# A graph network on one core: edge messages by outer products instead of per-edge matrices

## The reference, cut to what matters

```python
eh  = relu(e_feat @ en1_w.T + en1_b)            # (edges, 128), once
w_e = (eh @ en2_w.T + en2_b).reshape(-1, 32, 32)
for _ in range(6):
    msg = einsum('ei,eio->eo', out[src], w_e)
    agg = segment_sum(msg, dst) + conv_bias
    out = h = gru_cell(relu(agg), h)
```

## Time and profile before

| | us |
|---|---|
| median of 3 runs | 42728.8 (42723.92 to 42729.68) |
| the profiled execution's own time | 42514.04 |
| its span | 42512.1 |

### The profile page before, as it was taken

One profiled execution on the slowest core, in us unless ns is written; L12 is line 12 of the kernel. 1 busy time (PEld: TensorE's weight loads), 2 busy tenths in 40 slices (PEclk: granted clock), 3 DMA queues, 4 the chain that ended last, 5 costly groups with the idle time before them and its releaser, 6 DMA issues. The chain is left out here.

```text
span 42512.1 us, 515826 instructions
## 1 busy us (share of the span) xinstructions
PE 30160.5 (71%) x99425; PEld 18121.0 (43%) x99426; DVE 29047.4 (68%) x63440; ACT 11318.4 (27%) x26426; POOL 30972.7 (73%) x31499
## 2 busy tenths in 40 slices
PE   5222234444465222249999999999999999999999
PEld 5332323333365222234444444444444444444444
DVE  7333322221155222249999999999999999999999
ACT  0000001111110000014444444444444444444444
POOL 1666655555503665669998999899899989998997
PEclk8555556655555555569999999999999999999999
DMA  1110012210031010011111111111111111111111
GB/s 45 41 41 24 20 35 62 62 34 21 21 76 23 12 12 12 12 25 46 46 45 44 46 45 45 45 46 45 44 46 45 46 44 46 45 46 44 45 46 42
DMA packets 1365766, 1669.90 MB, mean 39 GB/s; under 512 B 847196, under 2 KB 1012047, under 8 KB 1252303
## 3 DMA queue, kind: packets, MB, share of 16 engines
q1 hardware_dynamic: 664232, 1115.69, 8.2%
q0 software_dynamic: 669696, 495.09, 7.3%
q10 hardware_dynamic: 31680, 57.69, 0.4%
HBM read 1393.98 MB, written 274.47 MB: 39 GB/s over the span
## 5 line engine op out<-in xcount | busy, mean ns | idle before, releaser
L1706 PE MATMUL l3m_p_w<-en,l3m_hid 128*128 128x512 f32 x42240 | 20965.3, 619 | 656.8 <-DVE l3m_prod L1772 398.8
L1756 DVE TENSOR_REDUCE l3m_xg<-l3m_prod 128x32 f32<-128x1024 f32 x10560 | 12858.1, 1218 | 168.6 <-POOL l3m_prod L1637 0.8
L1628 POOL DMA_INDIRECT l3m_xg<-wide_table,l3m_mt x10560 | 10341.0, 979 | 2395.8 <-issue 2033.1
L1637 POOL TENSOR_TENSOR l3m_prod<-l3m_rest,l3m_xg 128x384 f32<-128x384 f32 x10560 | 10673.0, 1011 | 281.9 <-ACT l3m_rest L1683 93.7
L1706 PEld LDWEIGHTS l3m_p_w<-en,l3m_hid 128*128 128x128 f32 x42240 | 7164.5, 189 | 6865.7 <-issue 5224.6
L1683 ACT COPY l3m_rest<-l3m_p_w 128x384 f32<-128x384 f32 x10560 | 5050.6, 478 | 12815.6 <-PE l3m_p_w L1706 12187.2
L1768 DVE TENSOR_TENSOR l3m_prod<-l3m_p_w,l3m_xg 128x512 f32<-128x512 f32 x10560 | 7196.1, 681 | 429.2 <-PE l3m_p_w L1706 257.4
L1718 PEld LDWEIGHTS l3m_p_sum<-l3m_xg,l3m_apart 128*125 128x125 f32 x21120 | 3965.2, 188 | 5090.7 <-issue 2742.2
L1671 ACT ACTIVATE l3m_apart<-iota_lo,l3m_mt 128x125 f32<-128x125 f32 x10560 | 4238.6, 402 | 0.5 <-DMA l3m_mt<-dst_meta 0.5
L1718 PE MATMUL l3m_p_sum<-l3m_xg,l3m_apart 128*125 128x64 f32 x21120 | 3473.9, 246 | 23.0 <-DVE l3m_xg L1756 23.0
L858 POOL DMA_INDIRECT l2a_xg<-table,l2a_mt x1760 | 1676.7, 953 | 2443.5 <-DMA l2a_mt<-dst_meta 1896.8
(11 more groups left out here) (328 smaller groups left out, 22546.9 us busy)
## 6 DMA issues: line engine op xcount, KB each, us to landing
l3m_hid<-hid_t SPq DMA_DIRECT2D x660, 1024.0 KB
l3m_xg<-wide_table,l3m_mt POOLq DMA_INDIRECT x10560
hid_t<-l_hid SPq DMA_DIRECT2D x110, 1024.0 KB, 4.1
order_src_bk<-dst_bucket SPq DMA_DIRECT2D x52, 808.0 KB
order_dst_bk<-src_bucket SPq DMA_DIRECT2D x52, 808.0 KB
by_dst<-order_src_empty SPq DMA_DIRECT2D x28, 1071.0 KB, 24.4
l_rec<-by_dst SPq DMA_DIRECT2D x110, 272.0 KB
l_xg<-table,l_mt POOLq DMA_INDIRECT x1760
```

Source lines behind the costliest of these rows:

```text
L1628: pool.indirect_dma_start(xg[s][:, j, 0:2 * D], None, wide_table[:, :], bass.IndirectOffsetOnAxis(ap=mt[s][:, j, 0:1].bitcast(I32), axis=0 ...
L1637: pool.tensor_tensor(o_i(prod[j % RING][:, OWN:HD]), o_i(rest[j % RING][:, :]), state_of(s, j, REST), ALU.mult).then_inc(pooled, 1)
L1706: ins = pe.matmul(p_w[j % 2][:, c * 512:(c + 1) * 512], hid[s][:, j * P:(j + 1) * P], en2[:, c * 512:(c + 1) * 512], start=True, stop=True)
L1756: dve.tensor_reduce(xg[s][:, j, 2 * D:3 * D], o_i(prod[j % RING][:, :]), AX, ALU.add).then_inc(msgs, 1)
```

## The change

**Keys.** Only the source's buckets are counted. DVE makes one `hit_b` of 1,600 values for each of the 104 groups, and PE makes four matmuls with 400 columns. The degree's count moves into the ordering by source, where DVE makes two one-hot arrays of each chunk (32 x 125 and 32 x 100 values) and PE 32 matmuls.

**Order by destination.** Edges are now ordered by (lo, bucket // 8), and each such group of eight nodes is padded to a multiple of 32 edges (a subtile). Four subtiles are a quad of 128 edges; there are 2,064 quads. A new `order_groups` finds the positions: for each pair of 128-edge columns, PE compares against a running count that stays in PSUM and that ACT copies out (seven matmuls a pair, two of them in float32 and five in bfloat16), and DVE makes the comparison matrices. New phases `groups` and `seg` make the groups' bases and matrices that join subtiles of one group.

**Layer 0's edge part** works on 24 quads a group and leaves the hidden values untransposed (`quad_eh`), a slot one-hot (`quad_hit`) and `quad_meta`: the source's number and a 32-column matrix that says subtile and slot.

**`l2a`, `l2b`** become `dst_sum`: 2,064 gathers in sets of six with four sets of buffers, one small matmul a quad into [32 features, 32 (subtile, slot)], and joins of 96 subtiles by three matmuls and a copy or two.

**`l3m`.** The message is taken apart the other way: for a subtile and a slot, the sum over edges of (state i) x (hidden k) is an outer product; `en2` is applied to that sum afterwards. At the core of it, on PE:

```diff
-                            for c in range(2):
-                                ins = pe.matmul(p_w[j % 2][:, c * 512:(c + 1) * 512], hid[s][:, j * P:(j + 1) * P],
-                                                en2[:, c * 512:(c + 1) * 512], start=True, stop=True)
...
+                            for q in range(2):
+                                for x in range(2):
...
+                                    for c in range(2):
+                                        rows = slice((2 * x + c) * SUB, (2 * x + c + 1) * SUB)
+                                        ins = pe.matmul(half(t, x)[:, c, :, q * SLOTS:(q + 1) * SLOTS],
+                                                        eh[k][rows, 2 * j + q, :], spread[(2 * t + q) % RING][rows, :, :],
+                                                        start=True, stop=True)
...
+                        def mix(k, n):
+                            for c in range(4):
+                                ins = pe.matmul(p_pair[c * D:(c + 1) * D, 0:PAIRS], en2_i[:, 4 * n + c, :],
+                                                outer[k % 2][:, 4 * n + c, :], start=n == 0, stop=n == D // 4 - 1,
+                                                skip_group_check=True)
```

```diff
+                            act.copy(outer_of(k, j)[:, 0], half(t, 0)[:, 0]).then_inc(act_moved, 1)
...
+                            act.copy(outer_of(k, j)[:, 2:4], half(t, 1)).then_inc(act_moved, 1)
...
+                                dve.tensor_tensor(spread[(2 * t + q) % RING][:, :, :],
+                                                  xg[k][:, 2 * j + q, 0:D][:, :, None].broadcast_to([P, D, SLOTS]),
+                                                  p_hit[:, at:at + SLOTS][:, None, :].broadcast_to([P, D, SLOTS]),
+                                                  ALU.mult).then_inc(spreads, 1)
...
+                            dve.tensor_copy(outer_of(k, j)[:, 1], half(t, 0)[:, 1]).then_inc(dve_moved, 1)
```

For two quads ACT moves 512 and 1,024 values a partition out of PSUM, DVE 512, and DVE makes two spreads of 256. Once in 24 quads (a block) DVE transposes 768 values by 32x32 blocks (`turn`), PE joins 96 subtiles with the running total (`join`, four matmuls of 256 columns), and ACT copies and stores the total. POOL is left with the gathers:

```diff
+                        with pool.Fori(0, NBLK) as b:
+                            for k in range(SETS):
+                                pool.wait_ge(meta_in[k], b * 16 + 16)
+                                pool.sem_inc(begun, 1)
+                                for j in range(SET):
+                                    pool.indirect_dma_start(
+                                        xg[k][:, j, :], None, wide_table[:, :],
+                                        bass.IndirectOffsetOnAxis(ap=mt[k][:, j, 0:1].bitcast(I32), axis=0)).then_inc(rows_in[k], 16)
+                        sums.collect(pool)
```

In `order_groups` the chunk's keys go to all 128 partitions, ahead of the records of the chunk before:

```diff
+                        def keys(c, s):
+
+                            sp.wait_ge(keys_free, c + 1)
+                            sp.sem_inc(begun, 1)
+                            sp.dma_start(lrow[s][:, :],
+                                         chunk(dst_lo16, c)[None, :].broadcast_to([P, CHUNK])).then_inc(keys_in[s], 16)
```

More of the change, by code:

```diff
@@ L45 @@
 EPS = 1e-5
-PLACE = 32
 W = NB * D
@@ L246, in _, with find @@
                 def _(dve):
[L247 to L251, removed]
+                    dve.memset(nought[:, :], 0.0).then_inc(cleared, 1)
+                    def find(n, s):
                         dve.wait_ge(counted, n + 1)
[L255 to L259, removed]
@@ new lines, in _ @@
+                        fetch(0, 0, True)
+                        fetch(0, 1, True)
+                        with nc.allow_non_contiguous_dma(reason="one word of each subtile's first record"):
+                            for c in range(4):
+                                sp.dma_start(sub_key.rearrange("(q c) -> c q", c=4)[c:c + 1, :],
+                                             by_dst[c * SUB:c * SUB + 1, 0:NQ, 1]).then_inc(keys_kept, 16)
+                        with sp.Fori(0, NI - 1) as i:
+                            for s in range(2):
+                                fetch(i + 1, s, True)
+                                net.store(sp, i, s)
@@ new lines, in block_of @@
+                        def block_of(b, first=False):
+                            for k in range(SETS):
+                                if k == 2 and not first:
+                                    act.wait_ge(sums.turns, b)
+                                if k == 3 and not first:
+                                    sums.take_total(act, act.copy, b)
+                                if k >= 2 or not first:
+                                    take(b, k)
+                                for j in range(TWOS):
+                                    move(b, k, j)
+                                    if j == 0 and k == 3 and not first:
+                                        sums.store(act, b)
@@ L1740, in _ @@
+                        sums.start_act(act)
+                        act.sem_inc(act_moved, ACT_MOVED)
+                        act.sem_inc(taken, TAKEN)
+                        block_of(0, first=True)
+                        with act.Fori(1, NBLK) as b:
+                            block_of(b)
+                        take(NBLK, 0)
+                        take(NBLK, 1)
+                        sums.take_total(act, act.copy, NBLK)
+                        sums.store(act, NBLK)
                     @block.vector
@@ new lines, in block_of @@
+                        def block_of(b, first=False):
+                            for t in range(TB):
+                                if t == 0 and not first:
+                                    move(b - 1, TB - 2)
+                                    move(b - 1, TB - 1)
+                                if t == 0:
+                                    mark(b)
+                                if t >= 2:
+                                    move(b, t - 2)
+                                if t == 5 and not first:
+                                    dve.wait_ge(taken, b * SETS + TAKEN)
+                                    sums.turn(dve, b)
+                                spread_out(b, t // TWOS, t % TWOS)
@@ new lines, in _ @@
+                        sums.start_dve(dve)
+                        dve.sem_inc(spreads, SPREADS)
+                        dve.sem_inc(dve_moved, DVE_MOVED)
+                        block_of(0, first=True)
+                        with dve.Fori(1, NBLK) as b:
+                            block_of(b)
+                        move(NBLK - 1, TB - 2)
+                        move(NBLK - 1, TB - 1)
+                        dve.wait_ge(taken, NBLK * SETS + TAKEN)
+                        sums.turn(dve, NBLK)
```

1264 lines of the change are left out of this document (903 added, 361 removed).

## The result

On one chip the changed kernel took 51,308.6 us (median of 4 runs), the kernel before 42,726.4: a ratio of 1.201 [1.199, 1.203]. The profiled execution took 51,262. The forecast was 35,870.

The account below looks back on a forecast made before the run. POOL's gathers were taken to bound `l3m`; -6,770 there, with the small terms, summed to -6,863, so 42,514 became 35,651, and 215 for the median gave 35,870 us. The case spanned 34,800 to 37,000, the range went to 42,000.

Parts of the forecast that it names:

- Late instructions: Rival: PE's instructions come late in long loop bodies; 1.6 to 2.2 us a quad or ordering doubles, 38,000 to 46,000; chance 0.10.
- Strips abreast: PE in `l3m`: matmuls in four separate strips run at once, so PE needs 1.03 us a quad, not 3.6.
- weight loads: Rival: in `l3m`, PE's loads into different strips may not overlap; 1.5 us a quad, total 38,500; chance 0.24.
- halves keep order: Rival: float32 matmul halves start in program order, only two abreast in `l3m`; 1.9 us a quad, total 43,500; chance 0.12.
- one after another: Rival: strips of no use in `l3m`, PE's matmuls run serially; 3.6 us a quad, total 64,000; chance 0.03.
- POOL bounds `l3m`: Layer 3's message stage: gathers 1.285 us apart decide, 2,712 us a step, 1,128 less than before, 6.77 ms in all.
- `l2a` and `l2b`: Layer 2's sums: 2,064 gathers at 1.25 us plus 50 give 2,630 against 2,686; -110 us together.
- Keys: Keys stage: one of DVE's three compares stays, an iteration falls from 5.92 to 1.8 us; -428 us over 104.
- Ordering by source: Ordering by source: DVE gains 7.9 us a chunk, up to 410 us, partly in time already lost; +130 us taken.
- Ordering by destination: Ordering by destination: scatters running through save 500 us, against a longer broadcast and late PE instructions; 0 taken.
- `groups` and `seg`: New phases: a 3.2 MB broadcast, three passes over 8,256 values and 172 small instructions; +215 us.
- Layer 0: Layer 0: last 24 of 110 groups lose the edge part, the first 86 have half as much again; +150 us.

Follow-up runs that it names:

- `h2_pool_plain`: Changed kernel with layer 3's gathers replaced by plain loads of 128 rows that GpSimd issues itself after the first block: 32,549 us where before took 39,866.
- `h1_half_gathers`: Changed kernel gathering only the first, third and fifth quad of each set in layer 3 after the first block: 32,558 us where before took 39,866.
- the single pacing: Changed kernel with each layer 3 gather waiting for TensorE to be half a pair of quads further on: 33,871 us, and 46,644 where before took 42,529.
- the two paced forms: Changed kernel with layer 3's gathers made to wait for TensorE, two by two (46,405 us) or one by one (46,644 us).

## Why the prediction was wrong

- **The step that failed** is the one on PE: "If four strips run abreast it needs 0.43 + 0.43 + 0.17 = 1.03", with POOL beside it at 1.285, the larger of the two deciding. On H they don't lie beside each other. What a row of gathers does to PE was put at nothing. PE and its handovers take 1.24 us a quad (2,559 / 2,064, shown without gathers, and 0.21 above the 1.03), and 2.44 beside the gathers, so a gather costs 1.20 more. That this is close to the 1.25 from one gather to the next is no rule: part of it is the low clock behind each burst, and rows of two cost next to nothing. The rival *Late instructions* had the mechanism. Its chance of 0.10 and its 1.6 to 2.2 us a quad were both too low, and 46,000 as its end too: its own sum with 2.2 gives 12,384 x 2.2 + 360 = 27.6 ms and a total of 47,200.
- **Its evidence was misread.** Late matmuls stood in the earlier trace rows; I blamed the length of the loop and the broadcast, and held against them that before's `l3m` loop is longer and shows few. The F chip has the loop and the broadcast and no late matmul. What before's `l3m` lacks is gathers in a row (1,740 of the 1,759 intervals in a step are 2.17 to 2.25 us), and an engine that needs 16 weight loads a us. The Trainium skill (Runtime: NRT & Kernel Launch, Instruction fetch mechanics) says that engines fetch instructions by DMA in large blocks and that the cost of crossing into the next block is mostly hidden. On F the trace agrees, and nothing is late. On H instructions are late, and the trace doesn't name the path: the page of the profile counts 91 and 95 packets in the two instruction queues of after on H, and 91 and 94 on F.
- **Strips abreast: right.** 16 halves of `times` take 1.15 us at full clock, 24 of `mix` 1.18; one after another they would be 16 x 0.213 = 3.4 and 24 x 0.16 = 3.8. The rivals *weight loads*, *halves keep order* and *one after another* are out.

```profile
25001.75 1.18 PE L2355 MATMUL l3m_p_pair<-l3m_outer,en_i 128*32 128x192 f32 x24
25002.86 0.74 PEld L2340 LDWEIGHTS l3m_p_outer<-l3m_spread,l3m_eh 32*128 32x128 f32 x16 [0.30 <-issue]
25002.87 1.15 PE L2340 MATMUL l3m_p_outer<-l3m_spread,l3m_eh 32*128 32x256 f32 x16
```

- **POOL bounds `l3m`, 2,712 a step: right on F alone** (2,746), and so close by two errors of opposite sign: a gather took 1.25 us and not 1.285 (72 us a step less), waits and ends 170 and not 60. ACT's 0.59 and 1.02 and DVE's 0.41 and 0.69 are as forecast.
- **`l2a` and `l2b`: -110 forecast, +1,060 on H, +791 on F.** Their 2,630 is near F's 2,674. The error is on the side of before: "the other 486 us are waits of a double buffer" was 390 us of held-up work (2,670 against 2,279), which no wait per set takes away. On H signals come late too. In `l2a` ACT's copies wait for the matmuls of a set and the next matmuls for the copies. The last matmuls before a pause stand at 15,039.96, the next copy 17 us behind them, with a releaser that the profile calls remote; on F a copy follows its matmuls in 0.9 us (13,020.19 and 13,021.07):

```profile
15039.96 0.84 PE L1545 MATMUL l2a_p_pair<-l2a_mt,l2a_xg 128*32 128x32 f32 x12 [6.62 <-DMA l2a_xg<-table,l2a_mt]
15057.09 0.31 ACT L1572 COPY l2a_pairs<-l2a_p_pair 32x192 f32<-32x192 f32 x1 [20.14 <-remote]
```

- **Keys** -444 for -428. **Ordering by source** +81 on H and +1 on F, for +130. **Ordering by destination** +383 on H, +30 on F, for 0; 2,971 us stays just under the 3,000 that was to make the broadcast the culprit, and with the same broadcast the stage takes 2,316 on F. **`groups` and `seg`** +83 for +215. **Layer 0** +317 on H, +150 forecast, -32 on F; in another run of after on H the stage took 3,084, so 200 of the 317 are not steady.

The sum on H is 6 x 1,189 + 1,060 + 383 + 81 + 317 + 83 + 77 - 444 = 8,691 of 8,748 us. On F, from the two profiled executions on two chips, it is 6 x -1,111 + 791 + 30 + 1 - 32 + 83 - 4 - 444 = -6,241 of -6,139; the forecast was -6,863.

**What stays open:** what H and F chips differ in; by which path a row of gathers holds up PE's instructions and signals; whether any transfer that GpSimd issues does it (`h2_pool_plain` would tell, and ran on F only). That the length of a row decides is read from two traces; `h1_half_gathers`, which would test it by the total, ran on F only. No version that does all the work beats before on H; one that never lets more than two gathers follow each other was not run. On F the changed kernel is the fastest that does all the work, and the single pacing came out near it, 33,871 on another chip of the kind.

## What to carry to other kernels

When GpSimd's gathers will run back to back beside an engine that needs many short instructions, price both sums: the larger of the two, and the two added. The second was near here, 1.24 + 1.285 = 2.53 for 2.44, but only for rows of six; short rows with pauses cost less.

The profile of before had the sign, wherever GpSimd gathers or scatters without pause: `issue` ahead of PE rows, and waits put down to `remote`, where a signal came but the profile finds no instruction that had just ended. In `l2a`, on H and then on F:

```profile
DVE ACC L705 <- remote: 1558.0, 54, 39.2
DVE ACC L705 <- PE l2a_p_sum L904: 1336.7, 110, 23.1
```

In the whole profile of before DVE and ACT have 459 `remote` waits on H and none on F; in that of the changed kernel 5,696 and none. The spacing of gathers shows it too (2,670 / 1,760 = 1.52 us in `l2a` against a bare 1.25), but there POOL's waits had a name, `l2a_mt`, and the prediction took the name for the cause. The load that they waited for stood behind a `remote` wait of its own engine: in `l2a` SP has 55 of them ahead of it (L817) on H and none on F. And before a verdict on a large change, run it on more than one chip: here the same two kernels stand at 1.20 and at 0.85.

## What the hardware showed that was not expected

- On H a gather instruction of GpSimd (0.944 us, 1.25 from one to the next) costs PE 1.18 to 1.20 us of progress in bursts of six, and 0.84 to 0.86 in the two paced forms; behind rows of two PE keeps 80 of 82 weight loads. On F it costs none, in rows of up to 1,818. With 64 rows it is as dear as with 128. 128 rows of 256 bytes by SP's queue cost nothing.
- The late stretch begins some 3 us after the first gather of a burst: in the burst shown 53 weight loads come in the first 3 us, 21 in the next 5.6. PE may have that much in store; no run tests it.
- A gather of 64 rows takes GpSimd 0.90 us, of 128 rows 0.944, and a plain load that it issues 0.535.
- Four strips of 32 rows and four of 32 columns run abreast: 3.0 and 3.3 times faster than one after another, by the 1.15 us for 3.4 and the 1.18 for 3.8 above. From the Trainium skill's gains for strips (TensorE: Matmul & The Clock Gate, Measured speedup vs the span model) the prediction estimated 1.3 us a quad for all of PE's work; 1.24 was measured, handovers included. Its 0.6 for the column strips lies below what the page's 2.38, for three strips, would give: 1.71 / 2.38 = 0.72. The measured 1.18 us for 24 is 0.52 a quad.
